# One transformer layer on Trainium2: later input statistics, paired fold biases and a shorter hold for the last four tiles

## What is computed

```python
def _layernorm(x, axis=-1, eps=1e-5):
    ...
def _L0_attn_ref(x, Wq, bq, Wk, bk, Wv, bv, Wl, bl, Wo, bo):
    q = (x @ Wq + bq)                     # 16 heads of 64
    k = ((x @ Wk + bk) @ Wl + bl)
    v = ((x @ Wv + bv) @ Wl + bl)
    attn = softmax(q @ k.T / 8)           # per head, over 2048 keys
    return (attn @ v) @ Wo + bo
def _L0_ffn_ref(x, ...):                  # dense 1024 x 1024, shared rank 16,
    return base_out + shared_out + routed_out   # 6 routed experts of rank 16, top 2
x = x + _layernorm(_L0_attn_ref(_layernorm(x, axis=-1), ...), axis=-1)
x = x + _layernorm(_L0_ffn_ref(_layernorm(x, axis=-1), ...), axis=-1)
```

## Time and profile before

| | |
|---|---|
| median of 3 executions | 1413.39 us (1412.29 to 1520.67) |
| the profiled execution | 1412.82 us |
| its span, first to last instruction, slowest core (core 4) | 1411.3 us |
| spans of the other cores | 1407.9 to 1410.2 us |
| busy share of PE, ACT, DVE, POOL | 93%, 74%, 50%, 31% |

### The profile page before, as it was taken

One profiled execution on the slowest core, in us unless ns is written; L12 is line 12 of the kernel. 1 busy time (PEld: TensorE's weight loads), 2 busy tenths in 40 slices (PEclk: granted clock), 3 DMA queues, 4 the chain that ended last, 5 costly groups with the idle time before them and its releaser, 6 DMA issues.

```text
span 1411.3 us, 43965 instructions; the slowest of 8 cores (1407.9 to 1411.3 us)
## 1 busy us (share of the span) xinstructions
PE 1317.9 (93%) x17392; PEld 818.0 (58%) x17392; DVE 705.3 (50%) x1679; ACT 1042.0 (74%) x1138; POOL 433.5 (31%) x598
## 2 busy tenths in 40 slices
PE   6899999999999999999998999989999999998883
PEld 2456666666666666665555655555555555555551
DVE  0562434323332323232335676677777667667665
ACT  0367777777777777777777888878888888887651
POOL 5220101000010100000004555555556555465633
PEclk9999999999999999999999999999999999999997
DMA  9950112202020110123852212321222221222011
GB/s 131 232 162 6 54 30 73 64 17 59 15 62 19 47 43 26 25 78 92 113 114 64 77 59 72 121 71 60 77 78 82 91 77 45 86 69 86 23 62 45
DMA packets 67129, 98.90 MB, mean 70 GB/s; under 512 B 30208, under 2 KB 43904, under 8 KB 66416
## 3 DMA queue, kind: packets, MB, share of 16 engines
q1 hardware_dynamic: 56944, 83.03, 19.5%
q0 software_dynamic: 9984, 13.06, 6.8%
HBM read 76.56 MB, written 32.57 MB: 77 GB/s over the span
## 4 chain that ended last, share of the span: by engine, by line
PE 76%; DVE 7%; issue 5%; ACT 5%; DMA 3%; POOL 2%; DVEq 0%; SPq 0%; POOLq 0%; ACTq 0%
PE fb L379 34%; PE sc L1122 17%; PE av L1154 15%; ACT p_sb L1139 4%; PE fb L431 4%; DMA wvT_sb<-wvT 2%; DVE gt L896 1%; PE sc L379 1%; DVE x L812 1%; PE fb L853 1%; DMA xst<-x 1%; PE fb L776 1%; PE sc L1124 1%; POOL wl_sb L67 1%; PE fb L324 1%
## 5 line engine op out<-in xcount | busy, mean ns | idle before, releaser
L1139 ACT ACTIVATE p_sb<-sc 128x1024 bf16<-128x1024 f32 x1024 | 991.0, 1021 | 261.3 <-PE sc L1124 258.2
L1154 PEld LDWEIGHTS av<-v_sb,p_sb 128*128 128x128 bf16 x8192 | 320.8, 97 | 97.1 <-issue 2.3
L1122 PE MATMUL sc<-q_sb,k_sb 64*128 64x256 bf16 (+1 forms) x2176 | 330.6, 265 | 16.0 <-ACT p_sb L1139 14.5
L1154 PE MATMUL av<-v_sb,p_sb 128*128 128x65 bf16 x8192 | 340.1, 193 | 0.5 <-issue 0.5
L1124 PE MATMUL sc<-q_sb,k_sb 64*128 64x256 bf16 (+1 forms) x2176 | 332.8, 266 | 0.0
L1122 PEld LDWEIGHTS sc<-q_sb,k_sb 64*128 64x128 bf16 x2176 | 149.6, 94 | 82.8 <-issue 46.8
L266 POOL TENSOR_SCALAR rsa<-sta 128x1 f32<-128x1 f32 x32 | 7.3, 227 | 523.9 <-DVE sta L261 357.4
L1124 PEld LDWEIGHTS sc<-q_sb,k_sb 64*128 64x128 bf16 x2176 | 146.3, 94 | 0.0
L379 PE MATMUL fb<-wo_sb,ut 128*128 128x512 bf16 x496 | 136.1, 381 | 4.9 <-DVE gt L890 3.3
L379 PE MATMUL fb<-bw_sb,x3fm 128*128 128x512 bf16 x480 | 135.6, 383 | 1.0 <-DVE x3fm L251 0.9
L379 PE MATMUL fb<-xfm,wq_sb 128*128 128x512 bf16 x512 | 129.5, 381 | 0.0
(11 more groups left out here) (172 smaller groups left out, 1478.5 us busy)
## 6 DMA issues: line engine op xcount, KB each, us to landing
xst<-x SPq DMA_DIRECT2D x64, 512.0 KB, 5.2
out<-y_sb SPq DMA_DIRECT2D x31, 512.0 KB, 3.1
urow<-u_scr SPq DMA_DIRECT2D x30, 256.0 KB, 5.2
u_scr<-u SPq DMA_DIRECT2D x64, 64.0 KB, 2.1
q_scr<-kq SPq DMA_DIRECT2D x32, 128.0 KB, 2.5
q_sb<-q_scr SPq DMA_DIRECT2D x4, 1024.0 KB, 8.3
u_scr<-u_sb SPq DMA_DIRECT2D x7, 512.0 KB, 3.6
wkT_sb<-wkT POOLq DMA_DIRECT2D x8, 256.0 KB, 11.6
```

What stands on the lines that cost most here:

```text
L1122: t.matmul(sc[slot][:, ci * w:(ci + 1) * w], k_sb[0:64, j, c * 128:(c + 1) * 128], qa[0:64], start=True, stop=True, tile_position=(0, 0))
L1139: exp_tok[g] = P.op("S", lambda a: a.activation(ps[:], sc[slot][:], AF.Exp, bias=-SHIFT, scale=1.0), tok, av_tok.get(g - 4))
L1154: r = t.matmul(av[u % 2][:, o:o + 65], ps[:, p0:p0 + 128], v_sb[:, j, c * 130 + h * 65:c * 130 + (h + 1) * 65], start=(s == 0 and h == 0 a ...
```

## The change

The statistics of input tiles 0 and 1 are called after the fold groups 0 and 1, and no longer ahead of the first one; tiles 0 to 11 are then transposed after groups 3 to 14, one after each, where before they came in threes after groups 1 to 3, 5 to 7, 9 to 11 and 13 to 15. `fold_bias` takes K's and V's bias in one multiplication with two moving columns (64 multiplications in all, before 128) and is called only ahead of the fold groups. For the last four tiles `ln3` and `tr3` are held 2 double steps, before 3, and the exponentials of the gate are put in 1 double step after `h_group`, before 2.

```diff
-        def fold_bias(n, h):
-
-            c0 = 0 if n == "k" else 8
+        def fold_bias(h):
+
             b = next_bank(True)
             pa = bank(b)
+            cols = bkvb[:].rearrange("p (a k) -> p k a", a=2)
 
             def mm(t):
                 for mo in range(4):
                     o = h * 512 + mo * 128
                     for k in range(NCH):
-                        r = t.matmul(pa[:, mo:mo + 1], wl_sb[:, k, o:o + 128], bkvb[:, c0 + k:c0 + k + 1],
+                        r = t.matmul(pa[:, 2 * mo:2 * mo + 2], wl_sb[:, k, o:o + 128], cols[:, k, :],
                                      start=(k == 0), stop=(k == NCH - 1))
                 return r
             tok = P.op("T", mm, w_row if h else w_row[:NCH], w_tok["bkv"], bfree[b])
-            o = c0 + 4 * h
-            ev = P.op("V", lambda v: v.tensor_tensor(bklc[:, o:o + 4], pa[:, 0:4],
-                                                     bcols[:, 24 + 4 * h:28 + 4 * h], ALU.add), tok, c_tok)
-            bfree[b] = ev
-            w_tok["b%sl%d" % (n, h)] = ev
+            for i, n in enumerate("kv"):
+                o = 8 * i + 4 * h
+                w_tok["b%sl%d" % (n, h)] = P.op("V", lambda v, i=i, o=o: v.tensor_tensor(
+                    bklc[:, o:o + 4], pa[:, 0:8].rearrange("p (m a) -> p a m", a=2)[:, i, :],
+                    bcols[:, 24 + 4 * h:28 + 4 * h], ALU.add), tok, c_tok)
+            bfree[b] = w_tok["bvl%d" % h]
...
-        for i in range(2):
-            fold_bias("k", i)
-            ln0(i)
+        for h in range(2):
+            fold_bias(h)
         for g in range(2 * NCH):
             run(fold_group("v", wvT_sb, wvl_sb, g % NCH, g // NCH))
-            if g % 4:
-                tile0(3 * (g // 4) + g % 4 - 1)
-        for h in range(2):
-            fold_bias("v", h)
+            if g < 2:
+                ln0(g)
+            elif 2 < g < 15:
+                tile0(g - 3)
...
-                later(2, exps)
+                later(2 if n < NT - 4 else 1, exps)
...
+        def hold(n):
+            return 3 if n < NT - 4 else 2
+
         def t3_of(n):
-            return [(2.0, lambda: tr3(n), past(("x", n), 3))]
+            return [(2.0, lambda: tr3(n), past(("x", n), hold(n)))]
...
-            add(lambda n=n: ln3(n), 0.0, past(("z", n), 3))
+            add(lambda n=n: ln3(n), 0.0, past(("z", n), hold(n)))
...
-        add(lambda: ln3(c), 0.0, past(("z", c), 3))
+        add(lambda: ln3(c), 0.0, past(("z", c), hold(c)))
```

## The result

The changed kernel takes 1417.28 us (median of 10 runs, 1414.83 to 1419.1), the kernel before beside it 1413.20 us (10 runs): ratio 1.0031, 95% interval 1.0021 to 1.0041. That is 4 us slower, far less than 2% but clear of no change; forecast were 4 us faster, 1409.5, in a range of 1404 to 1415. The profiled execution took 1416.56 us, its span is 1415.0 us on core 6; the cores lie between 1410.3 and 1415.0, against 1407.9 to 1411.3 before.

What follows compares the result with a forecast made beforehand. TensorE, busy 93% of the span, was taken to bound the kernel. Start -4.4, loop's end +4.0 and tail -3.5 sum to -3.9 us: from 1413.39 to 1409.5 us, range 1404 to 1415.

Steps and rivals of the forecast that it cites:

- The first fold group at 50.5, set by wvT: Start of the V fold: group 0 waits for wvT's transfer, which the change does not move; 0 us.
- The biases, -1.74: Between fold and first keys group: V's bias multiplications leave TensorE's path, two-column ones cost nothing extra; 1.74 us saved.
- The order of the tiles, -2.7: V fold: later statistics and one tile per group bring the keys group earlier, 4.4 us together with the biases.
- The walk over TensorE, VectorE and ScalarE: V fold: a 0.4 us stall, then twelve transposition and group pairs at 2.17 us; first keys group at 85.4.
- as long as one load is still outstanding when the next is issued, the pace stands: V fold: x loads 6 to 10, issued 2 to 5 us later, still land 2.5 us apart, the delay hidden.
- a rival with 0.13: V fold: x loads bind, tiles 11 to 13 land 2.5 us later, only the biases' 1.7 gained; 1412 us, chance 0.13.
- The exponentials, +0.3: Near the loop's end: tile 28's earlier exponentials hold the softmax 1.7 us, mostly absorbed by the wait behind; 0.3 us left.
- The loop's end, +4.0: Last twelve double steps: new waits, 3.2 us of them at tile 30's transposition, and three more units; 4.0 us later.
- The last unit, 0: From the last exponential to the last tile's transposition: no change forecast, 0 us.
- the one on the other side: Rival, slower than before: waits at tile 30's transposition pass 7.6 us and the clock falls; 1413.5 to 1417 us, chance 0.17.
- The tail, -3.5: After the loop: GpSimd free earlier and tile 30's gate already done, so the tail is 3.5 us shorter.
- the last tile's chain starts 1.4 us earlier: Tail: with tile 29 gone from GpSimd, the last tile's scale starts sooner; 1.4 us if only this term counts.

Runs made afterwards that it cites:

- f2: Kernel before with only the K and V biases paired, old order of the tiles and old end; 1409.55 us, ratio 0.9987.
- f1: e1 with the two halves of wq's load issued behind fold groups 6 and 15 instead of at the beginning; 1409.19 us, ratio 0.9982.
- g3: e1 with tr_h of tiles 28 and 29 placed later and wq's halves loaded behind fold groups 11 and 15; 1410.07 us, ratio 0.9920.
- h3: g1 with wq's halves loaded behind fold groups 11 and 15; 1408.73 us, ratio 0.9965.
- g2: e1 with only the exponentials of the last four tiles one double step earlier; ratio 1.0023, mean over cores 1403.3 us.
- e4: Changed kernel with tile 28's exponentials put in two double steps after its product again; ratio 1.0108, mean over cores 1410.9 us.
- e3: Changed kernel with tile 30's second gate part behind the last attention unit, three units there left to the next call; ratio 1.0036, cores 1407.2 us.
- g1: e3 with tile 30's transposition alone held 3 double steps again; ratio 1.0051, mean over cores 1404.8 us.
- e1: Changed kernel with the old end, so the start of the change alone; ratio 1.0058, mean over cores 1403.7 us.
- h2: g4 with the last tile's z products issued ahead of tile 30's gate and tr_h; 1402.19 us, ratio 0.9922.
- g4: g3 with tr_h of tiles 24 to 27 placed later too; 1408.54 us, ratio 0.9934.

## Why the prediction was wrong, point by point

**The first fold group at 50.5, set by wvT.** Right: 50.1, with a wait for the transfer of wvT in front of it. Over all the kernels it lies between 48.7 and 50.7 as a mean of the cores, and not by their edits: the three kernels with the start of before or only its biases changed have 50.7, 48.9 and 49.05.

**The biases, -1.74.** Right: f2 measures -1.6. Two columns cost 29 ns where one cost 27, inside the wait for wvT. (The upper bound of 4.4 us was added up wrong: 8 in 0.61 make 4.9 for 64. It changes nothing.)

**The order of the tiles, -2.7.** Mostly wrong: 0.8 of it came, or 1.3 by the cores. The walk over TensorE, VectorE and ScalarE holds (f1, g3 and h3 come to 36.1, 35.3 and 35.0, the walk gives 34.9 behind the first group). The step that failed is "as long as one load is still outstanding when the next is issued, the pace stands". The pace of 2.5 us did stand, but the whole row of landings from load 6 on shifted by 2.8 to 2.3 us. wq's two halves were under way beside them, and without wq (f1) load 6 lands 5.1 us sooner; that they took just the turns that loads 6 to 10 had had fits this, and no run shows it more closely. I had named this as a rival with 0.13, said it would hit tiles 11 to 13, and it hit from 6 on. Here a load's landing went by when it was issued, and not only by the pace.

**The exponentials, +0.3.** Right in mechanism and size: 0.3 in g2, nothing beyond the spread in e4.

**The loop's end, +4.0.** Right: +4.1, or +3.9 with steps 496 to 500. The wait at tile 30's transposition was forecast at 3.2 and is 3.18, the copy behind it 0.94 for 0.9. tr_h(28) waits 1.1 to 1.5 for 1.6. tr_h(29) waits 1.1 to 1.4 for 2.4; what that saves the lower clock behind the stand takes (eight transpositions in 1.01 us for 0.61 in the rows above, and a clock of 0.50 to 0.57 over the next 4 us on every core), a term that the sum did not have. That two errors cancel there is argued from these rows; no run takes them apart.

**The last unit, 0.** Wrong, and this decides the sign: +3.5. The step reads "the last three of tile 29 and both gate parts of tile 30 come inside the loop", and I booked it as gain for the tail only. I had counted in which double step each piece is popped, and not asked what stands behind it in VectorE's list: in the last step that is the reciprocal for which TensorE waits. All that was needed for the price stood in the rows: the earlier trace rows shows 2.20 us for such an operation under GpSimd's addition, and the earlier trace rows 2.04. With the 3.5 in it the sum would have been -0.4 and, with the 2.0 by which the fold fell short, +1.6; what is left to the measured +3.4 is mainly the tail. Nor did one of the rivals have it: the one on the other side put the loss at tr3(30), whose wait is just as forecast.

**The tail, -3.5.** Wrong for the change: -0.8. The step that failed is "the last tile's chain starts 1.4 us earlier". GpSimd was free as forecast: it starts the last tile's scale 0.17 us behind the aggregated statistics (1385.53 and 1385.36), where before it took 1.58. But the statistics themselves come 8.6 us behind the transposition's start (1385.36 less 1376.77), against 7.1 before (1378.76 less 1371.68), and so do they on every core, 8.6 to 8.9 for 7.1. The sum had no term for the clock there: the transposition takes 1.01 us for 0.61 and the first half of z 2.77 for eight multiplications (later 1.89). The stand of 4.6 us lies in front of that, but it is not the whole cause, for e3 has no such stand and its clock falls all the same. Where the clock keeps 1.00 (four cores of g1, four of h3) the statistics come at 7.1 and the tail is 35.8 to 35.9, 3.3 to 3.5 below before: there the term has its full size. Where it falls, in the same two kernels, the tail is 38.8 to 39.8 and next to nothing is gained. So the mechanism was right and the clock took its yield; what decides on a core whether the clock falls behind the wait of 1.54 us no run shows. The held addition L891 of the earlier trace rows was to go; it went, to 0.16 us, but L870 three operations ahead of it is held 1.72 instead, by the same addition of tile 30 on GpSimd (1397.02 to 1399.36). A hold that was taken from one small operation fell on its neighbour, as GpSimd's addition lay where it lay.

**The holding of small operations.** The Trainium skill, SBUF — State Buffer, section "Who interferes with whom", has it that a VectorE operation with two SBUF inputs contends with a GpSimd one that reads SBUF, and that the one that comes second is blocked for the whole instruction. The traces agree to 0.03 us at L908, L870 and L891 (each ends as GpSimd's operation ends). L909 is held as well, 2.40 us, with one tensor and one scalar per partition as inputs; the same section names such operations among those that can take the shared ports, on conditions, and no run here tells which of them applied.

**What is not settled.** What decides on a core whether the clock falls behind the last unit, worth 3 to 4 us of the tail in g1 and h3. Where the 1.5 us lie by which e1 gains more over its cores than in the fold: steps 496 to 500 hold 1.0 of it (13.15 for 14.12), but they take 12.4 to 15.1 us from core to core within one kernel. And the 0.6 us of the start.

## What to carry to other kernels

When a piece of work is moved to an earlier place in an order written by hand, ask on each engine that it issues to what it now stands in front of, and whether the bound engine waits for that; a handful of 0.15 us operations cost 3.5 us here because they came to stand ahead of one reciprocal. A gate that stays shut costs what the bound engine could have done in that step (0.9 us here), an opened one costs the wait for late data (2.4 us more here): compare the two by number before opening it. And a gain in waits is only kept if the last item's own chain is issued first: h2 differs from g4 by one line, and that line is worth 5 us.

## What the runs showed of the hardware

A load issued 4.9 us later landed 2.8 us later, and with wq's loads out of the way its time from issue to landing fell from 9.1 to 3.9 us. A matrix multiplication with two moving columns started every 29 ns, with one every 27. Behind the stand of 4.6 us the granted clock was 0.50 on all eight cores, which is the lower level of 1.2 GHz, and eight transpositions took 1.01 us instead of 0.61. Behind that of 3.2 us, in front of tile 30's transposition, eight transpositions took 1.01 us on four cores and 0.61 to 0.96 on the others, and over the 4 us that followed the clock was 0.50 on seven cores and 0.57 on one. A wait of 1.5 us was followed by 0.50 on some cores and by 1.00 on others (g1, h3). In the stretch of the earlier trace rows the mean fell from 0.96 to 0.80. Small VectorE operations beside a long GpSimd one took 1.05 to 2.40 us instead of 0.17 to 0.23, and ended with it.
